# Perceiver block on one Trainium2 core: order of VectorE's side work and of its loads in the first cross attention

## The chip, the cores and the metric

One core of one Trainium2 chip runs the whole program. The metric is device time in microseconds (us) of one execution, taken as the median of several runs. Of the kernel before there are three runs: 1730.8 us in the median, from 1730.18 to 1734.52.

## What is computed

The reference is a chain of six stages on x (16 items of 64 tokens, 512 wide): cross attention, a time mixing attention, a feed forward net with 4 bit weights, a second cross attention, a sparse attention and a feed forward net with ternary weights. The change is in the first stage:

```python
x = x + _L0_xattn_ref(_layernorm(x), ctx_1024, ctx_1024, mask, Wq, bq, Wk, bk, Wv, bv, Wo, bo)
# _L0_xattn_ref, for each of the 16 items, 16 heads of 32, 64 queries, 512 context rows
q, k, v = split_heads(Q @ Wq + bq), split_heads(K @ Wk + bk), split_heads(V @ Wv + bv)
attn = softmax(einsum('bhqd,bhkd->bhqk', q, k) / sqrt(32) + mask * -1e9)
out = einsum('bhqk,bhkd->bhqd', attn, v) @ Wo + bo
```

Two pieces of other stages' work on weights are done beside it, since they depend on no activation:

```python
# first feed forward net: weights of 1408 x 512, in blocks of 16
scale = max(max(abs(wb)) / 6, 1e-12); wq = GRID[searchsorted(MID, abs(wb / scale))] * sign(wb) * scale
# second feed forward net: weights of 2048 x 512
scale = 1 / clip(mean(abs(w)), 1e-5)
```

## The kernel before

The stage is the function `projected_attention`. It goes over 16 items b (a "body" each). Every engine has its own program, written out by hand in its own order, and they meet by semaphores.

TensorE (`@block.tensor`, line 482) does for each body, in this order: `scores(b, 0)`, the four value projections of item b, with the second half product of item b-1, the transposes of context chunks 2 and 3 of item b+1 and the transposes of the first probabilities between them, then `scores(b, 1)`, `key(b+1, 0)`, `half_product(b, 0)`, `key(b+1, 1)`, `turn(b+2, 0)`, `turn_probabilities(b, 1)`, `key(b+1, 2)`, `turn(b+2, 1)` and `key(b+1, 3)`. In even bodies from 2 on, `out(.., 0)` stands ahead of `turn(b+2, 1)` and `out(.., 1)` behind `key(b+1, 3)`. A key or value step is 12 matmuls, since context and weights are split into an upper and a lower part.

Those steps share three PSUM banks in turn. `work_order` lists all uses, and `bank_for` makes use n wait until use n-3 has been emptied (`emptied`). For an odd body the uses are key 0, key 1, turn 0, key 2, turn 1, key 3, so `key(b+1, 3)` waits for the emptying of `turn(b+2, 0)`. A turn counts as emptied (`ctxt_ready`) once two engines have worked on it: VectorE's `context_parts` (lines 707 and 710: upper bits into the one buffer `w.upper`, then the lower part), and behind them ScalarE's `context_upper` (line 632), which copies the upper part to its place. In even bodies with an out, the use three ahead of `key(b+1, 3)` is `key(b+1, 2)`, emptied by ScalarE's `key_copy` (line 640).

ScalarE's order in a body is: `exponentials(b, 0)`, `sums_copy(b-1)`, `context_upper(b+1, 2)`, `turned_copies(b, 0)`, `context_upper(b+1, 3)`, `exponentials(b, 1)`, `key_copy(b+1, 0)`, `key_copy(b+1, 1)`, `context_upper(b+2, 0)`, `turned_copies(b, 1)`, `key_copy(b+1, 2)`, `context_upper(b+2, 1)`, `key_copy(b+1, 3)`. The next body's `scores(b+1, 0)` wait for all four key copies.

VectorE does `masked_scores` (line 718), `value_copy` (695), `finish_heads` (735), `context_parts`, `spread_sums` (724 and 728) and `add_out` (745). Between them it has side work:

- `quantising(b, s)`: steps of `Quantiser` on pieces of the 4 bit weights (128 x 704). Two bodies take 30 steps, five in a slot. Slots come in two kinds of five instructions: steps 0 to 4 of a piece (lines 156 to 164, called A here) and steps 5 to 9 (lines 166 to 173, called B). In slots s = 0 to 3 the kernel before does nothing, A, B, A in even bodies and B, A, B, nothing in odd ones.
- `magnitudes(b, s)`: the sum of absolute values of a ternary piece of 128 x 1024 (line 769) and a small addition (line 772). All three of a pair of bodies stand in the odd one, in slots 1, 2 and 3. They share one buffer, `abs_piece`.

SyncE issues the loads in one queue, each behind a wait: `piece(it, k)` stores a quantised piece, waits for the store and loads the next, `abs_load(n)` (line 445) waits for magnitude n-1, `mask_load(b+2)` waits for all masked scores of body b, and `context_load(b+3)` waits until the context of item b+1 has been split. After the last body the program has a barrier, and the next stage begins with a layer norm (line 215).

Of the kernel before, what the change touches and what calls it, by code (L numbers as in the profile page):

```python
# [178 lines left out]

WEIGHT_ROW = INTER0 * D // P  # L180
WEIGHT_PIECE = WEIGHT_ROW // 8
FIRST_SLOT, STEPS_A_SLOT = 1, 5

TERNARY_WEIGHTS = ['L1_ffn_w_gate', 'L1_ffn_w_up', 'L1_ffn_w_down']
INTER1 = 2048
# [166 lines left out]
def flat_weight(d, name):  # L352

    return d.ins[name].rearrange("a b -> (a b)").rearrange("(p n) -> p n", p=P)
# [4 lines left out]
DOUBLES = PAIRS // 2  # L359
# [24 lines left out]
def projected_attention(nc, g, d, w):  # L384
# [13 lines left out]
    W_STEPS, P_STEPS = 3 * Q_STEPS, Q_STEPS  # L398
# [4 lines left out]
    LAST = B - 1  # L403
# [12 lines left out]
    with nc.Block() as block:  # L416
        @block.sync
        def _(sp):
            def context_load(b):

                sp.wait_ge(ctxt_ready, CH * (b - 1))
                sp.dma_start(w.ctx[b % 2][:, :, :], ctx_dram[b]).then_inc(ctx_loaded[b % 2], 16)

            def mask_load(b):

                sp.wait_ge(masked, PAIRS * (b - 1))
                sp.dma_start(w.mask[b % 2][:, :], d.mask[b].partition_broadcast(P)).then_inc(mask_loaded[b % 2], 16)

            def pieces(it, k):

                part = slice(it * WEIGHT_PIECE, (it + 1) * WEIGHT_PIECE)
                return flat_weight(d, FP4_WEIGHTS[k])[:, part], d.fp4[k][:, part]

            def piece(it, k):

                sp.wait_ge(piece_step, it * W_STEPS + P_STEPS * (k + 1))
                sp.dma_start(pieces(it, k)[1], w.piece[k][:, :]).then_inc(piece_stored[k], 16)
                if it + 1 < BODIES:
                    sp.wait_ge(piece_stored[k], 16 * (it + 1))
                    sp.dma_start(w.piece[k][:, :], pieces(it + 1, k)[0]).then_inc(piece_loaded[k], 16)  # L440

            def abs_load(n):

                sp.wait_ge(abs_step, 2 * n)
                sp.dma_start(w.abs_piece[:, :], flat_weight(d, TERNARY_WEIGHTS[n % 3])[
                    :, n // 3 * ABS_PIECE:(n // 3 + 1) * ABS_PIECE]).then_inc(abs_loaded, 16)

            sp.wait_ge(w.mask_ready, 1)
            sp.dma_start(d.mask, w.mask_scaled).then_inc(mask_stored, 16)
            sp.wait_ge(mask_stored, 16)  # L450
            for b in range(2):
                sp.dma_start(w.mask[b][:, :], d.mask[b].partition_broadcast(P)).then_inc(mask_loaded[b], 16)
            sp.dma_start(w.Wo[:, :, :], chunked(d.ins['L0_xattn_Wo'])).then_inc(w.weight_loaded[2], 16)
            context_load(2)
            for b in range(B):
                it = b // 2
                if b % 2 == 1:
                    piece(it, 1)
                if b + 3 < B:
                    context_load(b + 3)  # L460
                if b + 2 < B:
                    mask_load(b + 2)
                if b % 2 == 0:
                    piece(it, 0)
                else:
                    abs_load(3 * it + 1)
                    abs_load(3 * it + 2)
                    piece(it, 2)
                    if it + 1 < BODIES:
                        abs_load(3 * it + 3)  # L470
            for k in range(3):
                sp.wait_ge(piece_stored[k], 16 * BODIES)
# [215 lines left out]
        def _(dve):  # L688
            quantise = Quantiser(nc, w.qtmp)

            def value_copy(b, p):

                bank, full, count = filled("value", b, p)
                dve.wait_ge(full, count)
                nc.vector.tensor_tensor(w.V[b % 2][:, p, :], bank[:, :], g.rows[:, 0, :], ALU.add).then_inc(value_ready, 1)  # L695

            def context_parts(b, c):

                if b >= B:
                    return  # L700
                bank, full, count = filled("turn", b, c)
                upper, lower = w.upper[:, :], w.ctxT_lower[b % 2][:, c, :]
                dve.wait_ge(full, count)
                if b + c > 0:

                    dve.wait_ge(ctxt_ready, CH * b + c)
                nc.vector.tensor_scalar(upper.bitcast(I32), bank[:, :].bitcast(I32), UPPER_BITS, None,
                                        ALU.bitwise_and).then_inc(ctx_upper, 1)
                dve.wait_ge(ctx_upper, CH * b + c + 1)
                nc.vector.tensor_tensor(lower, bank[:, :], upper, ALU.subtract).then_inc(ctx_lower, 1)  # L710

            def masked_scores(b, half):

                dve.wait_ge(mask_loaded[b % 2], 16 * (b // 2 + 1))
                dve.wait_ge(score_full, 2 * b + half + 1)
                for r in range(4):
                    p = 4 * half + r
                    nc.vector.tensor_tensor_reduce(w.prob[r][:, :], score[r][:, :], w.mask[b % 2][:, :], 1.0, 3e38,  # L718
                                                   ALU.add, ALU.min, w.negmax[:, p:p + 1]).then_inc(masked, 1)

            def spread_sums(b):

                dve.wait_ge(exp_done, b * PAIRS + PAIRS)
                nc.vector.reciprocal(w.rinv[:, :], w.rowsum[:, b % 2, :]).then_inc(inverted, 1)
                dve.wait_ge(inverted, b + 1)
                if b > 0:
                    dve.wait_ge(sums_turned, b)
                nc.vector.tensor_copy(w.spread[:, :].rearrange("p (h n) -> p h n", n=HD),
                                      w.rinv[:, :].unsqueeze(2).to_broadcast([P, PAIRS, HD])).then_inc(spread_done, 1)
# [16 lines left out]

            def quantising(b, s):

                it, k0 = b // 2, (b % 2 * 4 + s - FIRST_SLOT) * STEPS_A_SLOT
                for k in range(k0, k0 + STEPS_A_SLOT):  # L750
                    if not 0 <= k < W_STEPS:
                        continue
                    i = k // Q_STEPS
                    if k % Q_STEPS == 0:
                        dve.wait_ge(piece_loaded[i], it * 16 + 16)
                    if it + k > 0:
                        dve.wait_ge(piece_step, it * W_STEPS + k)
                    quantise(k % Q_STEPS, w.piece[i][:, :], w.piece[i][:, :], WEIGHT_PIECE).then_inc(piece_step, 1)

            def magnitudes(b, s):  # L760

                i = b % 2 * 4 + s - (2 * DOUBLES - 3)
                if i < 0:
                    return
                n = b // 2 * 3 + i
                dve.wait_ge(abs_loaded, 16 * (n + 1))
                if n > 0:
                    dve.wait_ge(abs_step, 2 * n)
                nc.vector.tensor_reduce(w.abs_part[:, i:i + 1], w.abs_piece[:, :], AX.X, ALU.add,
                                        apply_absolute_value=True).then_inc(abs_step, 1)  # L770
                dve.wait_ge(abs_step, 2 * n + 1)
                nc.vector.tensor_tensor(g.abs_sum[:, i:i + 1], g.abs_sum[:, i:i + 1], w.abs_part[:, i:i + 1],
                                        ALU.add).then_inc(abs_step, 1)
# [6 lines left out]
            for b in range(B):  # L780
                masked_scores(b, 0)
                value_copy(b, 0)
                if b > 0:
                    finish_heads(b - 1)
                quantising(b, 0)
                value_copy(b, 1)
                context_parts(b + 1, 2)
                value_copy(b, 2)
                context_parts(b + 1, 3)
                if b < LAST:  # L790
                    value_copy(b, 3)
                    quantising(b, 1)
                    magnitudes(b, 1)
                    masked_scores(b, 1)
                else:
                    masked_scores(b, 1)
                    value_copy(b, 3)
                    quantising(b, 1)
                    magnitudes(b, 1)
                spread_sums(b)  # L800
                quantising(b, 2)
                magnitudes(b, 2)
                context_parts(b + 2, 0)
                if b % 2 == 0 and b > 0:
                    add_out(b // 2 - 1, 0)
                context_parts(b + 2, 1)
                quantising(b, 3)
                magnitudes(b, 3)
                if b % 2 == 0 and b > 0:
                    add_out(b // 2 - 1, 1)  # L810
            finish_heads(LAST)
# [1687 lines left out]
```

## Time and profile before

| | |
|---|---|
| runs | 1730.18, 1730.8, 1734.52 us |
| profiled execution, its own time | 1731.69 us |
| its span, first to last instruction | 1729.9 us |
| PE busy | 1495.6 us, 86% of the span |
| PE weight load busy | 989.6 us, 57% |
| DVE busy | 1125.4 us, 65% |
| ACT busy | 584.3 us, 34% |
| POOL busy | 295.5 us, 17% |
| mean granted TensorE clock | 0.945 |

PE is TensorE, DVE VectorE, ACT ScalarE and POOL GpSimd. The bodies of the first cross attention run from 64.71 us (the scores of item 0) to 656.58 us (the last addition to x). PE is busy in over nine tenths of most slices there, and GpSimd has nothing to do. The granted clock is 1.00 where TensorE has its full speed of 2.4 GHz and 0.50 where it has 1.2 GHz. In the rows, an idle time in square brackets stands before the instruction that it precedes, with the instruction that ended it; L512 is line 512. In what follows, P is the start of `scores(b, 0)` on TensorE and S that of `scores(b, 1)`.

### The profile page before, as it was taken

What the parts mean: (1) busy time and instruction counts of PE and PEld (TensorE: products, weight loads), DVE (VectorE), ACT (ScalarE), POOL (GpSimd) and SP (SyncE); (2) the same over time, 40 slices, a digit from 0 to 9 for tenths busy, and PEclk for the clock granted to TensorE, in tenths of its full rate; (3) what the DMA queues carried; (4) which work ended last, traced back from release to release, by engine and by line L of the source; (5) the groups of instructions that cost most, each with busy time, mean ns of one, the idle gap of its engine ahead of it and who ended that gap; (6) DMA issues with size and microseconds to landing.
All of it is one profiled execution on the core that took longest, in us unless ns stands there. A gap on an engine that the chain in (4) does not pass through costs nothing. (4 is left out here: it accounts for less than half of the span.)

```text
span 1729.9 us, 33725 instructions
## 1 busy us (share of the span) xinstructions
PE 1495.6 (86%) x14116; PEld 989.6 (57%) x14130; DVE 1125.4 (65%) x2155; ACT 584.3 (34%) x1221; POOL 295.5 (17%) x185
## 2 busy tenths in 40 slices
PE   6999999999999976997675999998799996885786
PEld 3677776777777753344634444444466663675343
DVE  5475766767667666604876677673688884665575
ACT  2344434434433431231033111101566661144332
POOL 2200000000000000400010000000599982160000
PEclk9999999999999997999888999998899998898899
DMA  6222313232232214000005000000455511004001
GB/s 234 87 87 85 101 57 99 83 99 89 69 101 65 60 51 128 1 0 3 4 1 201 0 1 0 0 0 1 191 207 169 201 68 35 1 3 146 1 0 49
DMA packets 47910, 120.05 MB, mean 69 GB/s; under 512 B 10606, under 2 KB 15470, under 8 KB 43675
## 3 DMA queue, kind: packets, MB, share of 16 engines
q1 hardware_dynamic: 47770, 118.04, 20.2%
q8 instruction: 107, 1.75, 0.4%
q14 instruction: 33, 0.26, 0.0%
HBM read 100.95 MB, written 17.07 MB: 68 GB/s over the span
## 5 line engine op out<-in xcount | busy, mean ns | idle before, releaser
L1129 POOL TENSOR_TENSOR tm_mixed<-tm_mixed,XNT 128x512 f32<-128x512 f32 x16 | 21.8, 1381 | 652.3 <-DVE tm_mixed L1152 652.3
L512 PE MATMUL bank<-l0x_ctxT,l0x_upper_k 128*128 128x512 f32 x256 | 110.5, 432 | 24.0 <-ACT l0x_ctxT L632 18.8
L647 ACT ACTIVATE l0x_prob<-l0x_prob,l0x_negmax 128x512 f32<-128x512 f32 x128 | 91.0, 712 | 119.3 <-DVE l0x_negmax L718 119.3
L525 PE MATMUL bank<-l0x_upper_v,l0x_ctxT 128*128 128x512 f32 x256 | 106.1, 415 | 0.0
L514 PE MATMUL bank<-l0x_ctxT,l0x_lower_k 128*128 128x512 f32 x256 | 104.6, 408 | 0.0
L513 PE MATMUL bank<-l0x_ctxT_lower,l0x_upper_k 128*128 128x512 f32 x256 | 104.0, 406 | 0.0
L527 PE MATMUL bank<-l0x_upper_v,l0x_ctxT_lower 128*128 128x512 f32 x256 | 100.9, 394 | 0.0
L526 PE MATMUL bank<-l0x_lower_v,l0x_ctxT 128*128 128x512 f32 x256 | 100.6, 393 | 0.0
L718 DVE CUSTOM_DVE_ANT_0 l0x_prob<-bank,l0x_mask 128x512 f32<-128x512 f32 x128 | 80.7, 687 | 27.1 <-PE bank L540 27.1
L632 ACT ACTIVATE l0x_ctxT<-l0x_upper 128x512 fp32r<-128x512 f32 x60 | 38.1, 635 | 175.0 <-DVE l0x_ctxT_lower L710 175.0
L1042 DVE TENSOR_REDUCE l1x_negmax<-bank 128x1 f32<-128x512 f32 x128 | 82.3, 685 | 21.3 <-PE bank L931 20.8
L695 DVE TENSOR_TENSOR l0x_V<-bank,rows 128x512 f32<-128x512 f32 x64 | 44.2, 690 | 69.8 <-PE bank L527 69.8
L888 POOL TENSOR_SCALAR l1x_piece<-l1x_piece 128x1024 f32<-128x1024 f32 x24 | 87.2, 3632 | 2.0
L1005 ACT ACTIVATE l1x_prob<-bank,l1x_negmax 128x512 f32<-128x512 f32 x128 | 87.0, 688 | 1.3 <-DVE l1x_negmax L1042 1.3
L245 PE MATMUL bank<-ident,XN 128*128 128x128 f32 x192 | 35.0, 368 | 56.4 <-DVE XN L225 56.4
L1626 PE MATMUL bank<-f_gateT,f_x 128*128 128x512 f32 (+1 forms) x192 | 82.3, 572 | 1.4 <-ACT f_x L1664 1.4
L1070 DVE COPY l1x_PT<-bank 128x512 f32<-128x512 f32 x112 | 72.7, 683 | 12.5 <-PE bank L942 12.5
L1672 ACT ACTIVATE f_silu<-bank 128x512 f32<-128x512 f32 (+1 forms) x24 | 13.5, 561 | 196.7 <-PE bank L1626 196.7
L1650 PE MATMUL bank<-f_downT,f_hT 128*128 128x512 f32 x176 | 78.6, 603 | 1.2 <-ACT f_hT L1682 1.2
L1626 PE MATMUL bank<-f_upT,f_x 128*128 128x512 f32 (+1 forms) x192 | 79.5, 557 | 0.0
L512 PEld LDWEIGHTS bank<-l0x_ctxT,l0x_upper_k 128*128 128x128 f32 x256 | 50.0, 195 | 50.3 <-ACT l0x_ctxT L632 20.5
L942 PE MATMUL bank<-ident,l1x_prob 128*128 128x128 f32 x512 | 68.3, 277 | 2.1 <-ACT l1x_prob L1005 2.0
(269 smaller groups left out, 3309.9 us busy)
## 6 DMA issues: line engine op xcount, KB each, us to landing
l0x_ctx<-in_ctx SPq DMA_DIRECT2D x16, 1024.0 KB, 4.8
l1x_ctx<-in_ctx SPq DMA_DIRECT2D x16, 1024.0 KB, 5.8
fp_weight<-l0x_weight_piece SPq DMA_DIRECT2D x24, 352.0 KB, 2.2
f_raw<-fp_weight SPq DMA_DIRECT2D x3, 2816.0 KB, 17.9
ternary_weight<-l1x_piece_out SPq DMA_DIRECT2D x24, 256.0 KB, 6.1
f_raw<-ternary_weight SPq DMA_DIRECT2D x3, 2048.0 KB, 14.0
l0x_abs_piece<-in_L_ffn_w_gate SPq DMA_DIRECT2D x8, 512.0 KB, 3.9
l0x_mask<-mask_scratch SPq DMA_DIRECT2D x16, 256.0 KB, 3.7
```

The costliest lines, as they stand in the source:

```text
L512: nc.tensor.matmul(bank[:, :], w.upper_k[:, kc, cols], c, start=kc == 0, stop=False)
L513: nc.tensor.matmul(bank[:, :], w.upper_k[:, kc, cols], c_lower, start=False, stop=False)
L514: last = nc.tensor.matmul(bank[:, :], w.lower_k[:, kc, cols], c, start=False, stop=kc == CH - 1)
L525: nc.tensor.matmul(bank[:, :], c, w.upper_v[:, kc, :], start=kc == 0, stop=False)
L526: nc.tensor.matmul(bank[:, :], c, w.lower_v[:, kc, :], start=False, stop=False)
L527: last = nc.tensor.matmul(bank[:, :], c_lower, w.upper_v[:, kc, :], start=False, stop=kc == CH - 1)
L647: nc.scalar.activation(w.prob[r][:, :], w.prob[r][:, :], ACT.Exp, scale=-1.0, bias=w.negmax[:, p:p + 1], accum_out=w.rowsum[:, b % 2, p:p ...
L718: nc.vector.tensor_tensor_reduce(w.prob[r][:, :], score[r][:, :], w.mask[b % 2][:, :], 1.0, 3e38, ALU.add, ALU.min, w.negmax[:, p:p + 1]). ...
L888: nc.gpsimd.tensor_scalar(part, part, WHOLE - 1, WHOLE + 1, ALU.max, ALU.min).then_inc(piece_step, 1)
L1005: nc.scalar.activation(w.prob[2 * (k % 2) + i][:, :], score[2 * (k % 2) + i][:, :], ACT.Exp, bias=w.negmax[:, p:p + 1], accum_out=w.rowsum ...
L1042: nc.vector.tensor_reduce(w.negmax[:, p:p + 1], score[2 * (k % 2) + i][:, :], AX.X, ALU.max, negate=True).then_inc(max_ready, 1)
L1626: last = nc.tensor.matmul(bank[:, 0:n], w.x[:, kc, :], weight[:, kc, at:at + n], start=kc == 0, stop=kc == CH - 1)
```

## The change

Only VectorE's order and SyncE's order of issue in the first cross attention are touched; all sums are the same.

- `quantising` now has three slots in every body: A, B, A in an even one and B, A, B in an odd one. Slot 0 stands behind `finish_heads`, as before. Slot 1 stood ahead of `masked_scores(b, 1)` and now stands behind `spread_sums(b)`. Slot 2 stood ahead of `context_parts(b+2, 0)` and now stands behind it. Slot 3 is gone. In the last body, slot 1 stands ahead of `value_copy(b, 2)`.
- `magnitudes`: one in an even body, two in an odd one. The first of each body stands behind `context_parts(b+1, 3)`, ahead of the last value copy; the second of an odd body stands behind slot 2, ahead of `context_parts(b+2, 1)`.
- SyncE: each body issues one `abs_load` ahead of its mask load, and odd bodies one more at their end, as before.

```diff
-FIRST_SLOT, STEPS_A_SLOT = 1, 5
+STEPS_A_SLOT = 5
@@ SyncE, body b, it = b // 2
                     context_load(b + 3)
+                abs_load(3 * it + 1 + b % 2)
                 if b + 2 < B:
                     mask_load(b + 2)
                 if b % 2 == 0:
                     piece(it, 0)
                 else:
-                    abs_load(3 * it + 1)
-                    abs_load(3 * it + 2)
                     piece(it, 2)
@@ quantising
-                it, k0 = b // 2, (b % 2 * 4 + s - FIRST_SLOT) * STEPS_A_SLOT
+                it, k0 = b // 2, (b % 2 * 3 + s) * STEPS_A_SLOT
@@ magnitudes
-                i = b % 2 * 4 + s - (2 * DOUBLES - 3)
-                if i < 0:
-                    return
+                i = b % 2 + s
@@ VectorE, body b
                 quantising(b, 0)
                 value_copy(b, 1)
                 context_parts(b + 1, 2)
+                if b == LAST:
+                    quantising(b, 1)
                 value_copy(b, 2)
                 context_parts(b + 1, 3)
+                magnitudes(b, 0)
                 if b < LAST:
                     value_copy(b, 3)
+                masked_scores(b, 1)
+                if b == LAST:
+                    value_copy(b, 3)
+                spread_sums(b)
+                if b < LAST:
                     quantising(b, 1)
+                context_parts(b + 2, 0)
+                quantising(b, 2)
+                if b % 2 == 1:
                     magnitudes(b, 1)
-                    masked_scores(b, 1)
-                else:
-                    masked_scores(b, 1)
-                    value_copy(b, 3)
-                    quantising(b, 1)
-                    magnitudes(b, 1)
-                spread_sums(b)
-                quantising(b, 2)
-                magnitudes(b, 2)
-                context_parts(b + 2, 0)
                 if b % 2 == 0 and b > 0:
                     add_out(b // 2 - 1, 0)
                 context_parts(b + 2, 1)
-                quantising(b, 3)
-                magnitudes(b, 3)
                 if b % 2 == 0 and b > 0:
                     add_out(b // 2 - 1, 1)
```

## Rows read from the trace of the kernel before

**Rows 1.** Windows view, bodies 6 and 7: length; busy time (count) by engine; clock; DMA share, GB/s
```profile
284.57:321.58 37.01, 36.36 (x322) 28.39 (x322) 22.88 (x47) 15.20 (x33) 0.00 (x0) 1.00 0.21 72
321.58:359.35 37.77, 34.34 (x307) 26.27 (x307) 28.03 (x53) 14.97 (x33) 0.00 (x0) 0.95 0.33 102
```
**Rows 2.** Waits of TensorE, 60 to 660 us: total, times, longest
```profile
PE bank L512 <- ACT l0x_ctxT L632: 18.8, 7, 2.8
...
PE bank L512 <- ACT l0x_KT L640: 3.9, 6, 0.7
```
**Rows 3.** Timeline of PE, body 7 from its second scores: start, duration, instruction, [idle before]
```profile
337.88 1.11 PE L540 MATMUL bank<-l0x_KT,XN 32*64 32x512 f32 x16
...
345.79 0.60 PE L498 MATMUL bank<-ident,l0x_ctx 128*128 128x128 f32 x4
...
353.97 0.50 PE L512 MATMUL bank<-l0x_ctxT,l0x_upper_k 128*128 128x512 f32 x1 [2.65 <-ACT l0x_ctxT L632]
...
359.35 1.12 PE L540 MATMUL bank<-l0x_KT,XN 32*64 32x512 f32 x16 [0.78 <-ACT l0x_KT L640]
```
**Rows 4.** Timeline of DVE over the same stretch
```profile
337.99 0.69 DVE L695 TENSOR_TENSOR l0x_V<-bank,rows 128x512 f32<-128x512 f32 x1 [1.19 <-PE bank L527]
...
342.59 0.69 DVE L718 CUSTOM_DVE_ANT_0 l0x_prob<-bank,l0x_mask 128x512 f32<-128x512 f32 x1
...
346.73 0.52 DVE L166 TENSOR_SCALAR l0x_qpow<-l0x_qxn 128x704 int32<-128x704 int32 x1
...
350.51 1.21 DVE L769 TENSOR_REDUCE l0x_abs_part<-l0x_abs_piece 128x1 f32<-128x1024 f32 x1
...
351.84 0.69 DVE L707 TENSOR_SCALAR l0x_upper<-bank 128x512 int32<-128x512 int32 x1
352.57 0.69 DVE L710 TENSOR_TENSOR l0x_ctxT_lower<-bank,l0x_upper 128x512 fp32r<-128x512 f32 x1
...
360.68 0.69 DVE L718 CUSTOM_DVE_ANT_0 l0x_prob<-bank,l0x_mask 128x512 f32<-128x512 f32 x1 [3.22 <-PE bank L540]
```
**Rows 5.** Timeline of ACT over the same stretch
```profile
353.29 0.63 ACT L632 ACTIVATE l0x_ctxT<-l0x_upper 128x512 fp32r<-128x512 f32 x1 [5.89 <-DVE l0x_ctxT_lower L710]
...
358.61 0.69 ACT L640 ACTIVATE l0x_KT<-bank,columns 128x512 f32<-128x512 f32 x1 [1.65 <-PE bank L514]
```
**Rows 6.** Windows, last key step to next scores: bodies 7, 11, sum of seven odd
```profile
353.97:359.35 5.38, 4.60 (x12) 3.13 (x13) 2.77 (x4) 3.67 (x7) 0.00 (x0) 0.68 0.64 208
...
503.44:507.25 3.81, 3.03 (x13) 2.18 (x13) 2.76 (x4) 3.68 (x7) 0.00 (x0) 1.00 0.55 204
...
sum 35.92, PE 30.47 PEld 21.53 DVE 19.34 ACT 25.72 POOL 0.00; mean PE 4.35 PEld 3.08 DVE 2.76 ACT 3.67 POOL 0.00
```
**Rows 7.** Timeline of PE, body 6, the last key step
```profile
316.87 0.50 PE L512 MATMUL bank<-l0x_ctxT,l0x_upper_k 128*128 128x512 f32 x1 [0.65 <-ACT l0x_KT L640]
```
**Rows 8.** Timeline of DVE, last body (15) to the end of the stage
```profile
627.32 0.68 DVE L695 TENSOR_TENSOR l0x_V<-bank,rows 128x512 f32<-128x512 f32 x1
...
631.28 0.69 DVE L718 CUSTOM_DVE_ANT_0 l0x_prob<-bank,l0x_mask 128x512 f32<-128x512 f32 x1 [0.53 <-PE bank L540]
...
648.52 1.22 DVE L769 TENSOR_REDUCE l0x_abs_part<-l0x_abs_piece 128x1 f32<-128x1024 f32 x1 [4.31 <-DMA l0x_abs_piece<-in_L_ffn_w_down]
...
649.86 0.42 DVE L735 TENSOR_TENSOR l0x_headsT<-bank,l0x_headsT 128x256 f32<-128x256 f32 x1
...
656.58 0.42 DVE L745 TENSOR_TENSOR X<-X,bank 128x256 f32<-128x256 f32 x1 [1.89 <-PE bank L584]
```
**Rows 9.** Timeline of ACT, the last copy of sums
```profile
640.18 0.38 ACT L662 ACTIVATE l0x_headsT<-bank 128x256 f32<-128x256 f32 x1 [1.56 <-PE bank L573]
```
**Rows 10.** Timeline of PE, an output step in body 6 and the last one
```profile
313.90 1.89 PE L584 MATMUL bank<-l0x_Wo,l0x_headsT 128*128 128x256 f32 x8
...
650.37 6.17 PE L584 MATMUL bank<-l0x_Wo,l0x_headsT 128*128 128x256 f32 x16 [10.23 <-issue]
```
**Rows 11.** View of the tile abs_piece, its 24 loads
```profile
DMA to landing us min/median/max: 3.6/4.3/12.8
```

More of the change, by code:

```diff
@@ L747, in quantising @@
             def quantising(b, s):
-                it, k0 = b // 2, (b % 2 * 4 + s - FIRST_SLOT) * STEPS_A_SLOT
+                it, k0 = b // 2, (b % 2 * 3 + s) * STEPS_A_SLOT
                 for k in range(k0, k0 + STEPS_A_SLOT):
-                    if not 0 <= k < W_STEPS:
-                        continue
                     i = k // Q_STEPS
```

## The prediction

> **What bounds the kernel now.** I first took the waits of TensorE over the stage, then its windows by body, then the timelines of TensorE, VectorE and ScalarE side by side in one odd body, one even body and the last one. In odd body 7 TensorE is busy for 34.34 of 37.77 us [rows 1]. The missing 3.43 us are exactly two pauses: 2.65 us ahead of the last key step and 0.78 us ahead of the next scores [rows 3]. So TensorE sets the pace of the bodies, and what can be won is its pauses and its slow clock. The waits say how often: the 2.65 us pause seven times, in odd bodies 1 to 13, 18.8 us in all, and a pause of 0.65 us six times, in even bodies 2 to 12, 3.9 us in all [rows 2].
>
> Who ends the long pause? The key step waits for its bank, last used by `turn(b+2, 0)`. TensorE had filled it at 345.79 + 0.60 = 346.39. VectorE split it only at 351.84, ScalarE copied at 353.29, and TensorE went on at 353.97 [rows 3 to 5]. Between 346.39 and 351.84 VectorE was working off masked scores, B and a magnitude. The masked scores had started only at 342.59, since A and a magnitude stood ahead of them [rows 4]. VectorE is thus late with one step by its order, not by its load (28.03 of 37.77 us busy).
>
> The clock belongs to this. From the last key step to the next scores, body 7 takes 5.38 us at a mean granted clock of 0.68, body 11 takes 3.81 us at 1.00 [rows 6]. The fall from 2.4 to 1.2 GHz comes behind the long pause; six of the seven odd bodies have it, body 11 has not. Together the seven stretches take 35.92 us [rows 6] against 7 x 3.81 = 26.67.
>
> The third place is the tail. `finish_heads` of item 15 could run once ScalarE has copied the sums, at 640.18 + 0.38. It runs at 649.86, because VectorE first does B and two magnitudes and stands 4.31 us in front of the last load of `abs_piece` [rows 8, 9].
>
> **Unit costs, from body 7** [rows 4]. A magnitude is 351.84 - 350.51 = 1.33 us. From value copy 3 to the masked scores behind it lie the copy, A and a magnitude, 342.59 - 337.99 = 4.60; the copy takes 0.61 to 0.69, so A is about 2.65. B is 350.51 - 346.73 = 3.78. From the start of masked scores to the first instruction behind `spread_sums` it is 346.73 - 342.59 = 4.14. Scores on TensorE to masked scores on a free VectorE take 360.68 - 359.35 = 1.33. The two context instructions end 1.42 after their start and let the next one go after about 1.34. Their start to ScalarE's copy is 353.29 - 351.84 = 1.45, the copy holds ScalarE about 0.55, and a key copy to the scores behind it is 359.35 - 358.61 = 0.74 [rows 3 to 5].
>
> **Odd bodies, new order.** All times from S. The first magnitude now lies behind `context_parts(b+1, 3)`, where VectorE waited 1.19 us for the last value projection [rows 4]; it fills that gap and overruns it by about 0.1 us, which ends ahead of the scores. Masked scores start at 1.33, instead of 342.59 - 337.88 = 4.71. Slot 1 (A) starts at 1.33 + 4.14 = 5.47 and ends at 8.12. `turn(b+2, 0)` is full at 345.79 + 0.60 - 337.88 = 8.51, so it is split at once and ScalarE has it copied at about 8.54 + 1.45 + 0.63 = 10.6. TensorE wants that bank behind its transposes, which ended at 353.97 - 2.65 = 351.32; less some 0.2 of overlap between two instructions (an estimate), the key step starts at 351.12 - 337.88 = 13.24. The long pause is gone, with 2.6 us to spare. As it ends, key 3 starts 353.97 - 351.12 = 2.85 us sooner (the pause and the overlap).
>
> What is late next? `context_parts(b+2, 1)`, and this is where the change doesn't do what it says: B and a magnitude now stand ahead of this chunk. B starts at 8.54 + 1.34 = 9.88 and ends at 13.66, the magnitude at 14.99, the chunk reaches ScalarE at 16.44 and holds it to 16.98. Queued behind it is `key_copy(b+1, 3)`, and all of the next scores wait for that: they start at 16.98 + 0.74 = 17.72. Without it they would start at 13.24 + 3.81 = 17.05 [rows 6]. So 0.67 us come back per odd body, and the pause ahead of the scores grows from 0.78 to 1.45. The bounds of this term are 0 (chunk and key copy just meet) and 2.0 (another 1.33, a magnitude's length, if one more thing slips); I take 0.67, since every link is a measured row.
>
> Sum: 7 x (2.85 - 0.67) = 15.3 us.
>
> **The clock.** A pause of 2.65 us or more was followed by a fall six times in seven, pauses of 0.65 us never: body 6 has 1.00 throughout [rows 1], and so have the other even bodies. The new 1.45 lies between and nearer to the short ones; I take no fall. That gives back 35.92 - 26.67 = 9.3 us. The bounds are 9.3 and, if all seven bodies still fall, -1.7. The Trainium skill speaks against my choice ("TensorE: Matmul & The Clock Gate", section "A second HAM failure mode: psum-queue depth-cycling"): there, small idle times between groups of matmuls that cycle through PSUM banks were enough to make the clock swing. By that rule the falls would stay; the trace agrees only for the long pauses.
>
> **Even bodies.** In an odd body masked scores come 4.71 - 1.33 = 3.38 us sooner, with A and a magnitude gone from ahead of them; in an even body only A was there, so they and all behind them on VectorE and ScalarE come 3.38 - 1.33 = 2.05 us sooner. The 0.65 us pause ahead of key 3, ended by a key copy that queues behind the context copy and the probability copies [rows 7], goes; with the overlap it is worth 0.65 to 0.9, I take 0.85. Six bodies: 5.1 us. Slot 0 has an A there now. Odd bodies have the longer B in that place, and TensorE has no other pause in them [rows 1, 3], so it costs nothing. The magnitude fills the gap ahead of value copy 3, as above. Slot 2 (A) runs while TensorE does key 2 and the output step. If that cover were gone, each would cost its own length, 2.66 or 1.33 us a body.
>
> **Loads and the queue of SyncE.** Each `abs_load` of 512 KB lands after 4.3 us in the median, 12.8 at most (the one at the start, beside all other loads) [rows 11]. The one that the second magnitude of an odd body needs is issued at about S and needed at S + 13.66: covered. The other two are issued a magnitude or a piece ahead of another body's first half. `abs_load` now stands ahead of `mask_load`, which waits for masked scores that come later anyway; `piece` and `context_load` keep their place. Their DMAs are the same in number. Cost 0; bounds 0 and, if landings took their maximum, still 0.
>
> **Tail.** In body 15 value copy 1, slot 1 (A), value copy 2 and the magnitude come ahead of masked scores: 627.32 + 0.61 + 2.65 + 0.61 + 1.33 = 632.5, against 631.28: 1.2 us later [rows 8]. The value copy behind it slips by 0.9 us (its idle time before gave 0.3; an estimate, 1.2 at most), and with it TensorE's half products; ScalarE's copy of the sums ends at 640.18 + 0.38 + 0.9 = 641.5. VectorE: 632.5 + 4.14 + B 3.78 + 1.33 = 641.8, no wait for a load, since it was issued after 632.5. `finish_heads` at 641.8 instead of 649.86: 8.1 us. The output matmuls ran at the low clock, 656.58 - 649.86 = 6.7 us to the last addition. The matmuls start 650.37 - 649.86 = 0.5 behind it, and at full clock a step of 8 takes 1.89 us where 16 took 6.17 [rows 8, 10]. So 0.5 + 2 x 1.89 = 4.3: 2.4 us more. TensorE's pause ahead of them shrinks from 10.2 to 1 us, so I take the full clock: 10.5 us, bounds 8.1 and 10.5.
>
> **Sum.** 15.3 + 9.3 + 5.1 + 10.5 = 40.2 us, of which 29.7 in the bodies. Nothing behind the stage changes. The profiled execution took 1731.69 us (span 1729.9 and 1.8 around it), 0.9 above the median of 1730.8. So 1731.69 - 40.2 = 1691.5 for it, 1690.6 for the median; I say **1690.5 us**.
>
> **Rivals.**
> - **The clock keeps falling** behind the 1.45 us pause. For it: the pause is twice the old short one and scores of narrow matmuls follow. Against it: body 11, and all even bodies. It costs 9.3 + 1.7 = 11 us at most, with the tail 13.4: 1696 to 1704 us. Chance 0.15.
> - **The wait moves on:** VectorE's work ahead of chunk 1 slips by another 1.33 us and the pause ahead of the scores takes it, 7 x 1.33 = 9.3 us, so 1700; half of it would be 1695. For it: B and a magnitude now stand there. Against it: the chain above has no unmeasured link. Chance 0.07.
> - **Slower:** the second magnitude of an odd body waits for its load, VectorE being in order, chunk 1 behind it, the key copy and the scores behind that. Each us of lateness costs seven. It eats all 40 us from 5.7 us of extra wait on, that is if the load landed 13.7 + 5.7 = 19.4 us after issue. The longest landing is 12.8. It would give 1731 and more. Chance 0.02.
> - **No change**, the pauses being taken by TensorE elsewhere: within 5 us of 1730.8. TensorE's busy time and pauses add up to the body, which speaks against it. Chance 0.03.
>
> **How the numbers follow.** The forecast has 0.73; its own range is 1685 to 1696, from 0 for the extra pause (4.7 us less) to one or two kept falls. To leave out no more than 2 in 10, the range goes to 1704: 1685 to 1704. A measurement of this kernel can tell about 0.3% (5 us) from no change. Faster by over 0.3%: 0.95, within 0.3%: 0.03, slower: 0.02.
>
> **What would show it.** Right: no wait of the key step on the context copy in odd bodies; a pause of about 1.45 us ahead of each even item's scores; no 0.65 us pauses; a clock of 1.00 through the bodies; scores of item 15 at about 587.6 instead of 617.29; `finish_heads` of item 15 without a wait for a load. A pair of bodies should take 70.2 us instead of 74.8. Wrong: falls of the clock behind the new pause, a VectorE wait on `abs_piece` in the bodies, or a pause over 2 us ahead of the scores.

## The result

The changed kernel takes 1692.78 us in the median of four runs (1690.14 to 1694.62), the kernel before, beside it, 1730.49. The ratio is 0.9777, with a 95% interval from 0.9756 to 0.9797. A second measurement gave 0.9769 (0.9753 to 0.9785). The forecast was 1690.5 us.

The profiled execution took 1693.05 us, span 1691.3. The windows view of both kernels, cut at the scores of item 0, the scores of item 15 and the transposes of the next layer norm, says where the 38.6 us between the two spans went. "Bodies" below means the first of the three stretches, "tail" the second. Before (start and end; length; busy time and count of TensorE, its weight loads, VectorE, ScalarE and GpSimd; clock, DMA share, GB/s):

```profile
64.71:617.29 552.58, 523.64 (x4630) 405.69 (x4629) 377.94 (x744) 227.28 (x495) 0.00 (x0) 0.98 0.25 81
617.29:665.00 47.71, 27.35 (x325) 20.64 (x324) 30.25 (x68) 12.26 (x28) 0.00 (x0) 0.79 0.22 69
665.00:1729.90 1064.90, 894.90 (x8992) 532.95 (x9006) 690.52 (x1296) 329.57 (x678) 276.28 (x171) 0.93 0.16 56
```

After:

```profile
62.70:584.63 521.93, 510.66 (x4630) 398.96 (x4629) 377.46 (x746) 229.19 (x495) 0.00 (x0) 1.00 0.25 86
584.63:621.77 37.14, 24.87 (x325) 18.86 (x325) 28.84 (x66) 12.26 (x28) 0.00 (x0) 0.93 0.23 73
621.77:1691.27 1069.50, 902.07 (x9006) 536.91 (x9006) 690.61 (x1296) 329.57 (x678) 276.62 (x171) 0.93 0.16 56
```

The bodies gave 552.58 - 521.93 = 30.65 us (forecast 29.7), the tail 47.71 - 37.14 = 10.57 (forecast 10.5). Ahead of the bodies lie 2.0 us less and behind the tail 4.6 us more, where nothing was changed; the last experiment is on that. VectorE's busy time in the bodies hardly moved (377.94 and 377.46): the same work, placed otherwise.

The waits of TensorE answer to [rows 2] (total, times, longest). Both lines of the key steps are gone, and what is left in the bodies stands ahead of the scores:

```profile
PE bank L539 <- ACT l0x_KT L639: 11.3, 8, 1.5
```

Body 7 after, on TensorE and VectorE, answers to [rows 3, 4] (S is 321.39 here):

```profile
321.39 1.11 PE L539 MATMUL bank<-l0x_KT,XN 32*64 32x512 f32 x16
...
334.24 0.60 PE L497 MATMUL bank<-ident,l0x_ctx 128*128 128x128 f32 x4
334.59 0.48 PE L511 MATMUL bank<-l0x_ctxT,l0x_upper_k 128*128 128x512 f32 x1
...
339.08 1.12 PE L539 MATMUL bank<-l0x_KT,XN 32*64 32x512 f32 x16 [1.50 <-ACT l0x_KT L639]
```

```profile
320.22 1.21 DVE L764 TENSOR_REDUCE l0x_abs_part<-l0x_abs_piece 128x1 f32<-128x1024 f32 x1
...
322.72 0.69 DVE L717 CUSTOM_DVE_ANT_0 l0x_prob<-bank,l0x_mask 128x512 f32<-128x512 f32 x1 [0.50 <-PE bank L539]
...
329.94 0.69 DVE L706 TENSOR_SCALAR l0x_upper<-bank 128x512 int32<-128x512 int32 x1 [0.36 <-PE bank L497]
...
335.05 1.21 DVE L764 TENSOR_REDUCE l0x_abs_part<-l0x_abs_piece 128x1 f32<-128x1024 f32 x1
...
336.38 0.69 DVE L706 TENSOR_SCALAR l0x_upper<-bank 128x512 int32<-128x512 int32 x1
```

Chunk 0 is split as soon as it is there: VectorE now waits 0.36 us for it, where TensorE used to wait for VectorE. The last key step follows its transposes by 0.35 us, without a pause. Chunk 1 (336.38) comes behind B and a magnitude, and its copy on ScalarE sits ahead of the last key copy:

```profile
337.83 0.63 ACT L631 ACTIVATE l0x_ctxT<-l0x_upper 128x512 fp32r<-128x512 f32 x1 [2.70 <-DVE l0x_ctxT_lower L709]
338.36 0.67 ACT L639 ACTIVATE l0x_KT<-bank,columns 128x512 f32<-128x512 f32 x1
```

The tail answers to [rows 8]; no instruction waits for a load any more:

```profile
607.76 1.21 DVE L764 TENSOR_REDUCE l0x_abs_part<-l0x_abs_piece 128x1 f32<-128x1024 f32 x1
...
609.09 0.42 DVE L734 TENSOR_TENSOR l0x_headsT<-bank,l0x_headsT 128x256 f32<-128x256 f32 x1
...
613.34 0.42 DVE L744 TENSOR_TENSOR X<-X,bank 128x256 f32<-128x256 f32 x1 [1.21 <-PE bank L583]
```

### The profile page after: what moved, and what is told of

Its sections match the earlier page's. It is cut to its first block and busy times, and to the rows that moved or that the text cites. A ratio compares the mean times of both kernels' runs of the same rounds, so it can differ in the third digit from the quotient of the medians.

```text
span 1691.3 us, 33739 instructions
## 1 busy us (share of the span) xinstructions
PE 1484.9 (88%) x14130; PEld 983.8 (58%) x14130; DVE 1123.6 (66%) x2155; ACT 586.0 (35%) x1221; POOL 295.9 (17%) x185
## 5 line engine op out<-in xcount | busy, mean ns | idle before, releaser
L511 PE MATMUL bank<-l0x_ctxT,l0x_upper_k 128*128 128x512 f32 x256 | 106.7, 417 | 1.3 <-PEq L264 1.3
L513 PE MATMUL bank<-l0x_ctxT,l0x_lower_k 128*128 128x512 f32 x256 | 100.7, 393 | 0.0
L512 PE MATMUL bank<-l0x_ctxT_lower,l0x_upper_k 128*128 128x512 f32 x256 | 100.2, 391 | 0.0
L925 PE MATMUL bank<-l1x_KT,XNT 32*64 32x512 f32 x512 | 70.1, 626 | 0.0
L245 PEld LDWEIGHTS bank<-ident,XN 128*128 128x128 f32 x192 | 33.1, 196 | 59.1 <-DVE XN L225 46.7
```

The costliest lines, as they stand in the source:

```text
L511: nc.tensor.matmul(bank[:, :], w.upper_k[:, kc, cols], c, start=kc == 0, stop=False)
L512: nc.tensor.matmul(bank[:, :], w.upper_k[:, kc, cols], c_lower, start=False, stop=False)
L513: last = nc.tensor.matmul(bank[:, :], w.lower_k[:, kc, cols], c, start=False, stop=kc == CH - 1)
```

## The experiments

The theory: what counts is when VectorE splits chunk 0 (bank of the last key step) and chunk 1 (ahead of the last key copy); all else on VectorE is covered. The rival theories put the gain on the quantising slots alone, on the magnitudes alone, or make the new pause TensorE's own. Beside it stood an open question: which pauses are followed by a fall of the clock.

### One half of the change at a time

**Magnitudes and loads moved, slots as before:**

```diff
+                abs_load(3 * it + 1 + b % 2)
                 if b + 2 < B:
                     mask_load(b + 2)
...
-                    abs_load(3 * it + 1)
-                    abs_load(3 * it + 2)
...
-                i = b % 2 * 4 + s - (2 * DOUBLES - 3)
...
+                i = b % 2 + s
...
                 context_parts(b + 1, 3)
+                magnitudes(b, 0)
...
                     quantising(b, 1)
-                    magnitudes(b, 1)
...
                 quantising(b, 2)
-                magnitudes(b, 2)
                 context_parts(b + 2, 0)
+                if b % 2 == 1:
+                    magnitudes(b, 1)
...
                 quantising(b, 3)
-                magnitudes(b, 3)
```

> The kernel before with only the magnitudes and their loads moved (one per even body, two per odd one; the second of an odd body behind context chunk 0); the quantising slots stay. My theory, that only the time at which chunk 0 is split counts: in odd bodies masked scores start 1.2 us sooner and chunk 0 has one magnitude less ahead of it, together 2.5 of the 2.85 us, so a pause of some 0.2 to 0.3 us is left, the clock no longer falls (9.3 us back), the tail gains 6.5 to 9. Sum 33 to 36: 1695 to 1698. Rival, that the change works through the quantising slots it moves: little gain, 1720 or more.

Measured: 1698.71 us, ratio 0.9787 (0.9771 to 0.9803), so 36.6 us less than the kernel before, which took 1735.3 us in the runs beside it. Bodies and tail:

```profile
64.60:589.12 524.52, 514.26 (x4629) 399.62 (x4628) 376.21 (x746) 228.06 (x495) 0.00 (x0) 1.00 0.25 86
589.12:630.47 41.35, 27.59 (x325) 20.81 (x325) 28.84 (x66) 12.25 (x28) 0.00 (x0) 0.85 0.20 65
```

The long pause is gone but for some 0.2 us: in body 7 the last key step starts 338.37 - 337.80 = 0.57 us behind its transposes, where the changed kernel has 0.35. The clock is at 1.00. The six short pauses of even bodies stay, with the slots where they were:

```profile
PE bank L511 <- ACT l0x_KT L639: 4.0, 6, 0.7
```

This half alone brings 552.58 - 524.52 = 28.06 us in the bodies, where the whole change brings 30.65, and 6.36 of 10.57 in the tail: 34.4 us, with 33 to 36 expected.

**Slots moved, magnitudes and loads as before:**

```diff
                 if b < LAST:
                     value_copy(b, 3)
+                    magnitudes(b, 1)
                 masked_scores(b, 1)
...
                 if b < LAST:
                     quantising(b, 1)
+                magnitudes(b, 2)
                 context_parts(b + 2, 0)
                 quantising(b, 2)
-                if b % 2 == 1:
-                    magnitudes(b, 1)
...
                 context_parts(b + 2, 1)
+                magnitudes(b, 3)
```

(against the changed kernel, which has the new slots; SyncE's order is that of the kernel before.)

> The changed kernel with magnitudes and loads as in the kernel before (three in odd bodies: ahead of the second masked scores, ahead of chunk 0, behind chunk 1); only the quantising slots are new. My theory: chunk 0 is still in time (the magnitude ahead of it may wait for its load, some 4 us after masked scores end, and the split ends about 1 us before the bank is wanted), chunk 1 is 0.3 us later than in the changed kernel, so the pause ahead of scores is about 1.85 us: 7 x 1.8 + clock 9.3 + even bodies 5.1 + tail 3 = 30, so 1701. The two halves then add up to much more than the whole, since each alone takes the long pause away. Rival, that the magnitudes carry it: 1720 or more.

Measured: 1712.82 us, ratio 0.988 (0.9862 to 0.9899). That is 22.5 us less than the 1735.3 us beside it, where 30 were expected; it isn't the rival's 1720 either. Bodies and tail, VectorE's waits for the loads, and its magnitude, chunk 0 and chunk 1 in body 7 (S is 325.43):

```profile
62.30:594.71 532.41, 512.54 (x4629) 399.13 (x4628) 377.31 (x744) 228.43 (x495) 0.00 (x0) 1.00 0.26 84
594.71:639.27 44.56, 27.63 (x325) 20.84 (x324) 30.19 (x68) 12.26 (x28) 0.00 (x0) 0.82 0.24 74
```

```profile
DVE l0x_abs_part L767 <- DMA l0x_abs_piece<-in_L_ffn_w_up: 11.2, 8, 3.5
```

```profile
335.50 1.22 DVE L767 TENSOR_REDUCE l0x_abs_part<-l0x_abs_piece 128x1 f32<-128x1024 f32 x1 [1.13 <-DMA l0x_abs_piece<-in_L_ffn_w_up]
...
336.83 0.69 DVE L707 TENSOR_SCALAR l0x_upper<-bank 128x512 int32<-128x512 int32 x1
...
341.94 0.68 DVE L707 TENSOR_SCALAR l0x_upper<-bank 128x512 int32<-128x512 int32 x1
```

```profile
344.64 1.12 PE L540 MATMUL bank<-l0x_KT,XN 32*64 32x512 f32 x16 [2.65 <-ACT l0x_KT L640]
```

The load of the magnitude ahead of chunk 0 is issued behind the mask load, at 330.44 or S + 5.0, and lands 1.13 us too late, so VectorE stands still. (In the changed kernel body 7 issues its load ahead of the mask load, at S + 0.3.) Chunk 1 comes at S + 16.51 instead of the 14.99 of the changed kernel. The pause ahead of the scores is 2.65 us, where 1.85 was expected. So the order of the loads isn't cosmetic. The code says more, though no run shows it: with the loads in their old order the moved magnitudes could not run at all. The load for the first magnitude of an odd body would be issued behind a mask load that waits for all masked scores of that body, and the magnitude now stands ahead of the second half of them.

In the bodies this half alone gives 552.58 - 532.41 = 20.2 us in this profile, which has no fall of the clock, and 17.5 in a second one below (bodies of 535.05 us), which has two. The two halves together would be 28.06 + 20.17 = 48.2 us, and the whole gives 30.65: each by itself takes away nearly all of the same long pause (with the slots alone the last key step of body 7 starts 0.70 us behind its transposes). In the tail they nearly add up: 6.36 + 3.15 = 9.5 against 10.57.

### The pause that the change leaves

**Changed kernel, the second magnitude behind chunk 1:**

```diff
                 quantising(b, 2)
-                if b % 2 == 1:
-                    magnitudes(b, 1)
                 if b % 2 == 0 and b > 0:
                     add_out(b // 2 - 1, 0)
                 context_parts(b + 2, 1)
+                if b % 2 == 1:
+                    magnitudes(b, 1)
```

> The changed kernel, with the second magnitude of odd bodies moved behind the split of context chunk 1. My theory: the 1.50 us pause ahead of the next item's scores is that magnitude and B standing ahead of chunk 1, whose copy holds up the last key copy. Without the magnitude the chunk reaches ScalarE 1.33 us sooner, before the key copy could start at all, so the pause goes back to 0.78 us in all seven odd bodies: 7 x 0.72 = 5.0 us faster than the changed kernel, about 1688. Rival: the pause is set by TensorE's last key step and ScalarE alone, or VectorE then comes late to the next masked scores: no change, 1693.

Measured: 1688.29 us (1685.64 to 1691.35), ratio 0.9729 (0.9714 to 0.9744), against 0.9777 and 0.9769 of the changed kernel. The kernel before took 1735.3 us beside it, 3 to 5 us more than beside the changed kernel, so the windows of the profiles are the better measure of the step between the two. Its waits and windows:

```profile
PE bank L539 <- ACT l0x_KT L639: 6.2, 8, 0.8
```

```profile
64.70:581.64 516.94, 510.72 (x4630) 398.92 (x4629) 377.44 (x746) 229.95 (x495) 0.00 (x0) 1.00 0.26 87
581.64:618.78 37.14, 24.87 (x325) 18.85 (x325) 28.84 (x66) 12.26 (x28) 0.00 (x0) 0.94 0.23 72
```

All eight pauses are 0.78 us again, and the bodies are 521.93 - 516.94 = 4.99 us shorter, with 5.0 expected. The magnitude ahead of chunk 1 was the whole of the pause that the change added.

**The same, and the last body's magnitudes moved:**

```diff
-                magnitudes(b, 0)
                 if b < LAST:
+                    magnitudes(b, 0)
                     value_copy(b, 3)
...
                 spread_sums(b)
+                if b == LAST:
+                    magnitudes(b, 0)
...
-                if b % 2 == 1:
+                if b % 2 == 1 and b < LAST:
                     magnitudes(b, 1)
...
             finish_heads(LAST)
+            magnitudes(LAST, 1)
```

> As e1, and in the last body the first magnitude behind spread_sums and the second behind finish_heads. My theory: masked scores of the last body start 1.3 us sooner, finish_heads then waits only for ScalarE's copy of the sums: 1.0 to 1.3 us faster than e1, about 1687. Rival: the second magnitude waits for its load and holds the last additions back: 0 to 3 us slower than e1.

Measured: 1685.3 us (1682.38 to 1687.14), ratio 0.9712 (0.9697 to 0.9726). Its tail takes 36.00 us where that of the kernel above takes 37.14, so 1.14 less. This is the fastest version. Bodies and tail together take 552.90 us against the changed kernel's 559.07, so 6.2 us or 0.4% less; by the medians of the runs it is 7.5 us (1685.3 against 1692.78), by the ratios 0.6 to 0.7%, with the reservation made above. The second reduction starts at 603.06 without a wait, behind `finish_heads` and beside the output matmuls:

```profile
602.72 0.42 DVE L734 TENSOR_TENSOR l0x_headsT<-bank,l0x_headsT 128x256 f32<-128x256 f32 x1
603.06 1.21 DVE L764 TENSOR_REDUCE l0x_abs_part<-l0x_abs_piece 128x1 f32<-128x1024 f32 x1
```

### Pauses and falls of the clock

**Changed kernel with a useless reduction ahead of chunk 1**, once over 1024 columns and once over 512:

```diff
+                if s == 1 and b < LAST:
+                    nc.vector.tensor_reduce(w.abs_part[:, 0:1], w.abs_piece[:, :], AX.X, ALU.add,
+                                            apply_absolute_value=True)
                 nc.vector.tensor_reduce(w.abs_part[:, i:i + 1], w.abs_piece[:, :], AX.X, ALU.add,
```

> The changed kernel with a second, useless reduction of 128 x 1024 ahead of context chunk 1 in seven odd bodies. The chain behind chunk 1 says that TensorE's pause grows by the whole 1.21 to 1.25 us, to 2.72: 7 x 1.22 = 8.6 us slower than the changed kernel if the clock holds, and up to 7 x 1.6 = 11 more if every pause is followed by a fall: 8.6 to 19.6 slower. Rival, that chunk 1 isn't what holds the scores: no change.

> As the kernel with the longer pause, but the useless reduction reads 128 x 512: about 0.65 us, so a pause of 2.15 us: 7 x 0.65 = 4.6 us slower than the changed kernel if the clock holds, up to 15.6 if falls follow pauses of this length too.

Beside them stood the changed kernel once more and a repeat of the one with only the slots new:

> The changed kernel itself, beside the others of this call, as their measure: 0.977 to 0.978 of the kernel before, pauses of 1.50 us ahead of the scores, no fall of the clock in the bodies.

> The kernel with only the slots new once more. Its first profile had seven pauses of 2.65 us and no fall of the clock, while its executions lay between 1709 and 1718 us with mean clocks from 0.950 to 0.945. Theory: whether a pause of 2.65 us is followed by a fall differs from execution to execution, with where in time the pauses lie; other executions, in profile or mean clock, show falls (1.6 us each), spread 5 to 10 us. Rival: it is the place that matters: a pause ahead of the scores is never followed by a fall, one ahead of the last key step is; then the profile shows none again and the mean clock stays at 0.950.

Measured side by side: changed kernel 1693.33 us, with 1024 columns 1708.15 (ratio to the kernel before 0.9857, 0.9838 to 0.9875), with 512 columns 1704.41 (0.9837, 0.9821 to 0.9853), slots alone 1715.71 (0.9914, 0.9891 to 0.9936). With 1024 columns that is 14.8 us slower than the changed kernel (8.6 to 19.6 expected), with 512 it is 11.1 (4.6 to 15.6). The seven pauses grew to 2.62 and 2.09 us, where 2.72 and 2.15 were expected; the first line is for 1024 columns, the second for 512:

```profile
PE bank L539 <- ACT l0x_KT L639: 19.2, 8, 2.6
```

```profile
PE bank L539 <- ACT l0x_KT L639: 15.4, 8, 2.1
```

The clock says the rest. Two windows of the kernel with 1024 columns, each from the scores behind such a pause on: at the first the clock falls, at the second it doesn't.

```profile
131.95:136.00 4.05, 4.05 (x24) 2.60 (x25) 2.53 (x8) 1.98 (x5) 0.00 (x0) 0.69 0.38 153
277.54:281.50 3.96, 3.96 (x28) 2.41 (x28) 2.53 (x8) 1.89 (x5) 0.00 (x0) 1.00 0.25 97
```

Counted over all profiles (stretches at 1.2 GHz within the bodies, seven pauses in each profile; the last line also has the one of body 0):

| pause, us | ahead of | kernel | followed by a fall |
|---|---|---|---|
| 2.65 to 2.89 | last key step | before, two profiles | 6 of 7, 6 of 7 |
| 2.65 | scores | slots alone, two profiles | 0 of 7, 2 of 7 |
| 2.62 | scores | with 1024 columns | 4 of 7 |
| 2.09 | scores | with 512 columns | 3 of 7 |
| 1.50 | scores | changed, two profiles | 0 of 7, 0 of 7 |
| 0.78 | scores | magnitudes alone, and the two with the second magnitude behind chunk 1 | 0 of 24 |

The pause's length alone doesn't decide: 2.65 us ahead of the scores was followed by no fall in one profile and by two in the next, of the same kernel. The two were taken on different chips, but the chip is not needed for a difference: on the first chip alone the four executions of this kernel lay between 1709.26 and 1718.05 us, with mean clocks from 0.950 to 0.945. The rival of the repeat, that a pause in this place is never followed by a fall, is refuted. A fall costs about 1.4 to 1.7 us, the length of a pair of bodies with a fall less that of one without. For the kernel with 1024 columns 7 x 1.12 = 7.8 us of pause and 4 x 1.55 = 6.2 of falls make 14.0, and its bodies took 535.84 us against 521.93, 13.9 more:

```profile
64.70:600.54 535.84, 516.69 (x4630) 401.82 (x4628) 385.47 (x753) 228.99 (x495) 0.00 (x0) 0.99 0.24 84
```

### The parts that the change doesn't touch

> The kernel before once more, for a second profile of it. Two questions. Falls of the clock behind the seven pauses of 2.65 us: theory of chance by where in time the pauses lie, some number from 2 to 7, not necessarily the 6 of the first profile; rival, always 6 or 7. And the part behind the first cross attention, from the transposes of the next layer norm to the end: 1064.9 us in the first profile of before, 1067 to 1070 in six profiles of other orders. Theory: this is scatter of the clock in later stages and comes out between 1065 and 1070 here; rival: the change itself makes the later stages slower, and it is 1065 again.

Measured: the kernel before in a second profile, span 1730.7 us, and its three stretches:

```profile
62.20:614.89 552.69, 523.70 (x4629) 405.75 (x4628) 378.12 (x744) 227.39 (x495) 0.00 (x0) 0.98 0.26 81
614.89:662.99 48.10, 27.78 (x326) 20.94 (x325) 30.27 (x68) 12.26 (x28) 0.00 (x0) 0.80 0.22 68
662.99:1730.70 1067.71, 901.79 (x8992) 539.86 (x9006) 690.61 (x1296) 329.91 (x678) 276.60 (x171) 0.93 0.16 56
```

The bodies repeat within 0.1 us, with six falls again, but not the same six: here the second long pause goes without, in the first profile the sixth. So the rival "always 6 or 7" ahead of the last key step still stands: two profiles are too few to refute it. The later stages took 1067.7 us instead of 1064.9, the part ahead of the bodies 62.2 instead of 64.7. Over nine profiles of other orders the later stages lie between 1065.5 and 1070.0. So the 2.0 us won ahead of the bodies and most of the 4.6 us lost behind them lie within what differs between executions of one kernel and between the other orders. That the changed kernel loses 1 or 2 us there for good is not excluded: its two profiles have 1069.5 and 1069.8. Nor is the cause of the scatter found: the clock has part in it at most. The second profile with only the slots new has 0.92 in this stretch and is among the shortest (1065.47 us), the first of the kernel before has 0.93 and 1064.90.

## Why the prediction was right

- **The bound.** TensorE's busy time plus its pauses made up the body, and this held after: body 7 takes 34.00 us, 32.51 busy and 1.50 in its one pause. So each pause could be priced at its full length, plus some 0.25 us of overlap between two instructions that a pause takes away as well: a key step follows its transposes by 0.35 us where nothing holds it up, and by 353.97 - 350.72 = 3.25 where the pause was 2.65.
- **The odd bodies, link by link.** Forecast and measured, from S: masked scores 1.33 and 1.33, chunk 0 split 8.54 and 8.55, chunk 1 14.99 and 14.99, ScalarE's copy 16.44 and 16.44, scores 17.72 and 17.69. The new pause was forecast at 1.45 and measured at 1.50. Moving the magnitude showed that the change misses its aim at chunk 1: 4.99 us.
- **Even bodies.** The six pauses of 0.65 us are gone; a pair of bodies takes 70.1 us (forecast 70.2). That they hang on the slots and not on the magnitudes is shown by the halves: with the magnitudes alone they stay, with the slots alone they are gone. Which slot it is, A ahead of the masked scores or B ahead of chunk 0, was not separated.
- **The clock.** Right in its result (no fall in the bodies of the changed kernel, so the 9.3 us came back), thin in its reason, and so in part luck. I had set "2.65 us falls, 0.65 us doesn't" and put 1.45 near the short ones, with no row between. Ahead of the scores the runs show no fall in 14 pauses of 1.50 us, 3 in 7 at 2.09 and 6 in 21 at 2.62 to 2.65, and different shares at one length. The rule of the Trainium skill ("TensorE: Matmul & The Clock Gate", section "A second HAM failure mode: psum-queue depth-cycling"), that small idle times between bank-cycled groups are enough, didn't come true for pauses up to 1.50 us, and did in part from 2.09 us on. These pauses come once or twice in a body; the section speaks of frequent ones, which no run here has.
- **The tail.** 10.57 against 10.5. `finish_heads` starts 24.46 us behind the scores of item 15 instead of 32.57, so 8.1 us sooner (forecast 8.1), and waits for nothing but VectorE's order. From there to the last addition it takes 4.25 us instead of 6.72, at full clock: 2.5 us (forecast 2.4).
- **What was off.** The bodies gave 0.9 us more than the sum. Some 0.3 of it are two of the seven long pauses, which lasted 2.84 and 2.73 us and not the 2.65 of body 7. Another 0.3 are the odd bodies (the key step follows its transposes 3.25 - 0.35 = 2.90 us sooner, and the scores follow it 0.68 later: 2.22 net and not 2.18), and 0.2 the even ones (1.25 us became 0.36, so 0.89 and not 0.85). The step "Nothing behind the stage changes" left out 2.0 us less ahead and 4.6 more behind in this pair of profiles. The code there is the same, but its time differs between executions by some microseconds, which belongs into the range and was not named. Together that is 4.6 - 2.0 - 0.9 = 1.7 of the 2.3 us between 1690.5 and 1692.78. The rest is that the profiled execution lies 0.3 us above its median and not 0.9 as before.
- **The slower rival** (a VectorE wait for a load ahead of a chunk) didn't occur, but was real: with the loads and magnitudes in their old order VectorE waits 1.1 us per odd body, and the chain puts all behind it, the next scores too, that much later.

## What to carry to other kernels

Where engines run in fixed orders, find the wait of the bounding engine, follow it back to the instruction that ended it, and look at what stood ahead of that instruction on its own engine; side work belongs behind such an instruction, and the load of side work must be issued early enough to let it move. After a move, list what is now behind the moved work: here the change fixed one chunk and left 5 us at the next. Two edits that each remove the same pause don't add up, so a change of several parts needs one run per part before any of them is given the credit. Here the magnitudes and their loads alone gave 34.4 of the 41.2 us in bodies and tail.

## What was not expected of the hardware

Behind pauses of 2.1 to 2.9 us TensorE's clock fell to 1.2 GHz only some of the times: 0, 2, 3, 4 and 6 of seven, each fall costing about 1.4 to 1.7 us, and the same kernel had none in one execution and two in another. Executions of the kernel with only the slots new lay between 1709 and 1722 us, those of the changed kernel, without such pauses, between 1690 and 1695. Whether the place of the pause matters (12 of 14 ahead of a key step, 6 of 21 ahead of the scores at 2.62 to 2.65 us) or only where in time it falls is left open.
